# The finishing stage of a graph network: normalisation on ScalarE, wide scaling, earlier weight loads, and moved edge keys

## The chip, the cores and the metric

The kernel runs on one core of a Trainium2 chip. The metric is the device time of one execution in microseconds, as the median of several runs: 5247.54 us for the kernel before, from three runs between 5239.28 and 5250.59 us.

## The reference

A graph of 6250 nodes with 256 features and 100,000 edges sorted by destination goes through two layers. Layer 0 is a graph attention convolution (softmax over the edges of each destination), a linear attention and a mixture of experts. Layer 1, where most of the change lies, is

```python
xn = _layernorm(x, axis=-1)
x = x + _L1_gnn_ref(xn, ...) + _L1_mix_ref(xn[None], ...)[0]
x = x + _L1_ffn_ref(_layernorm(x, axis=-1)[None], ...)[0]

h1 = relu(gcn_conv(embedding, W1, b1, src, dst, n))   # 256 -> 64
h2 = relu(gcn_conv(h1, W2, b2, src, dst, n))          # 64 -> 256
```

A `gcn_conv` multiplies by W, scales a row by `dinv[src] * dinv[dst]` per edge (`dinv` is one over the root of the degree plus one), sums over the edges of each destination, and adds the row's own term and the bias. `_L1_ffn_ref` sends every row to the one expert with the largest gate score, if that expert has a place left (capacity 1.25 times the mean, given out in row order), and scales by the softmax probability.

## The kernel before

The 6250 nodes stand in 49 blocks of 128 rows (`NB`, `P`). The sorted edges are cut in tiles of 128; where a tile covers several blocks, it is repeated once for each, so that every step has one block; there are 832 steps (`NS`), in groups of eight. The stages run one after another, each in a block with a queue of instructions per engine, all engines meeting at its end.

`edge_steps` finds the tile and the block of each step and gathers the source, destination and weight of its edges (`rs`, `rd`, `rw`, each 128 x 896 numbers). VectorE converts the destinations to floats (`fd`), SyncE stores them at L225 as the key rows `key_d`, VectorE subtracts the block's first row (`fl`, L370), and TensorE turns the tables. `project_nodes`, the next stage, begins on VectorE with a wait for nine weight loads, for the stored keys (`m.keyed`) and for three masks of GpSimd (L552 is the last). The keys are read in `score_edges` and compared with their neighbours in `normalise_edges`, where a maximum is taken over each run of edges with equal keys.

`convolve(1)` sums the second graph convolution. GpSimd gathers 782 tiles of source rows, one indirect DMA each (L1886), into a ring; TensorE multiplies them by one-hot matrices that VectorE makes (L2109, L1953), VectorE adds the sums into `m.agg` (L1964), and the mixing network's block work goes between, with one block load per block on SyncE (L1923), after the loads of its weights. VectorE first folds weights (`fold`).

`finish_and_route1` handles the 49 blocks in seven groups of seven (`G`), with these steps, all in program order on each queue:

- VectorE: `scale(k)` multiplies 64 sums by `dinv` into `us` (L2273), five blocks ahead; `finish(k)` takes the relu of the projected block and adds it to the residual rows (L2277); `stats(k)` (L2281); per group `variance`, `choose` for the group before (gate scores to mask, L2316 to L2329), `normalise` (reciprocal L2301, the token's copy L2304, seven normalisations into `disp`, L2308), `place` for the group before (ranks to slots, L2338 to L2361).
- TensorE: `turn(k)` four blocks ahead (L2434), `project(k)` (L2440), then for a block of the group before `turn_normal` (L2447) and one block later `gate` (L2457), and per group the rank and total matmuls of the mask (L2482, L2483).
- ScalarE: copies of turned sums (L2394), of turned normalised rows (L2400) and of the residual rows into `disp` (L2407), per group a square root (L2422) and the exponential of the gate's gaps (L2425). It also issues the loads of the first two experts.
- GpSimd: per group seven indirect DMAs (L2255) that scatter the rows of `disp`, which is double, to the experts' buffer. `disp` is written again when the scatters of the group two before have landed (`sent`).
- SyncE: first four loads (64 x 256 weights `w2` and its bias row, the gate's weights and bias), then the finished rows to the output.

TensorE starts when these four loads have landed. A prologue of four turned blocks and the first group have no gate work; the last turn of the loop (the tail here) has only gate work. I number the seams between groups 0 to 6: at seam g the variance and normalisation are of group g, and choice and placement of group g-1.

## Time and profile before

| | us |
|---|---|
| median of three runs | 5247.54 |
| the runs | 5239.28, 5247.54, 5250.59 |
| profiled execution, its own time | 5253.34 |
| its span in the profile | 5251.4 |
| mean granted TensorE clock, of 1 | 0.736 |
| finishing stage, first instruction to last scatter's issue | 4605 to 4764 |

The profile is of one execution. It gives busy time per engine (PE is TensorE's matmuls, PEld its weight loads, DVE VectorE, ACT ScalarE, POOL GpSimd, SP SyncE; a q behind the name is the queue's own work, such as issuing a DMA), and for each instruction its start, duration, and what ended the idle time before it. An idle time "issue" is one in which the engine waited for nothing that the profile shows. The granted clock is 0.50 when TensorE gets 1.2 GHz and 1.00 at 2.4 GHz.

### The profile page before, as it was taken

The numbers are of one execution on the slowest core, as the hardware profiler recorded it, in microseconds if no ns is written. First come the engines' busy times: TensorE is split into PE (matmuls) and PEld (weight loads), VectorE is DVE, ScalarE is ACT, GpSimd is POOL, SyncE is SP. The second block draws the span as 40 slices with busy tenths as digits, with TensorE's granted clock in tenths as the row PEclk, the third lists the DMA queues.
The fourth block names the chain that finished last, engine by engine and source line by source line (L and its number), as shares of the span: only waits on it lengthen the run. The fifth ranks groups of instructions, "written<-read, shape, count | busy, mean of one in ns | idle before, by whom it ended". The sixth has DMA issues, their size and how long they took to land. (4 is left out here: it accounts for less than half of the span.)

```text
span 5251.4 us, 62217 instructions
## 1 busy us (share of the span) xinstructions
PE 3522.0 (67%) x13908; PEld 2764.9 (53%) x13909; DVE 2526.5 (48%) x5949; ACT 1049.5 (20%) x2215; POOL 3048.2 (58%) x2894
## 2 busy tenths in 40 slices
PE   4866666665399975999655555554555555567998
PEld 3734444433277765888544444443444545455665
DVE  5477777777712553222643444444333333463444
ACT  0122222221199911332100000000000000042111
POOL 1177777777299944222277777776777777722111
PEclk9976677777699987999565666665555555567999
DMA  5398777777588863222511111112111111132221
GB/s 111 115 248 247 241 241 241 241 241 224 158 264 272 272 210 112 70 70 62 166 33 32 33 33 33 33 32 44 33 32 33 33 33 33 30 118 89 73 79 34
DMA packets 437408, 616.97 MB, mean 117 GB/s; under 512 B 104714, under 2 KB 315466, under 8 KB 437003
## 3 DMA queue, kind: packets, MB, share of 16 engines
q1 hardware_dynamic: 306767, 391.02, 23.6%
q0 software_dynamic: 107728, 200.97, 15.6%
q10 hardware_dynamic: 22812, 23.86, 1.7%
q8 instruction: 36, 0.59, 0.0%
q14 instruction: 65, 0.53, 0.0%
HBM read 418.38 MB, written 211.62 MB: 120 GB/s over the span
## 5 line engine op out<-in xcount | busy, mean ns | idle before, releaser
L1886 POOL DMA_INDIRECT big<-t_d,src_tiles x1564 | 1482.6, 948 | 622.9 <-issue 457.3
L2109 PE MATMUL v_bank<-big,v_oh 128*128 x3328 | 685.2, 392 | 914.5 <-POOLq L1882 855.5
L2109 PEld LDWEIGHTS v_bank<-big,v_oh 128*128 128x128 f32 x3328 | 651.8, 300 | 990.9 <-issue 990.8
L704 POOL DMA_INDIRECT big<-xl_d,src_steps x832 | 794.1, 954 | 261.0 <-issue 230.2
L815 PE MATMUL se_z_ps<-big,se_oht 128*128 x1664 | 687.7, 569 | 370.9 <-DVE se_z L744 326.5
L1964 DVE TENSOR_TENSOR big<-big,v_bank 128x64 f32 x1664 | 366.8, 220 | 1138.9 <-PE v_bank L2109 917.5
L815 PEld LDWEIGHTS se_z_ps<-big,se_oht 128*128 128x128 f32 x1664 | 424.2, 276 | 634.1 <-issue 555.2
L1134 POOL TENSOR_TENSOR ae_v<-ae_v,ex 128x2048 f32<-128x2048 f32 x104 | 380.6, 3673 | 109.8 <-DMA ae_v<-xj_d 108.7
L744 DVE TENSOR_TENSOR se_z<-se_z_ps,big 128x528 f32<-128x528 f32 x416 | 291.7, 701 | 279.9 <-DMA big<-xl_d,src_steps 268.7
L1176 PE MATMUL ae_sums<-ae_v,ae_oh 128*128 128x266 f32 x1664 | 396.2, 395 | 25.9 <-ACT ae_oh L1125 17.3
L1176 PEld LDWEIGHTS ae_sums<-ae_v,ae_oh 128*128 128x128 f32 x1664 | 309.1, 191 | 112.9 <-issue 60.7
L2555 POOL DMA_INDIRECT out<-e_y,e_idx x64 | 63.1, 986 | 422.5 <-DVE e_y L2598 407.9
L1631 POOL DMA_INDIRECT y_d<-e_y,e_idx x112 | 117.3, 1047 | 305.8 <-DVE e_y L1620 282.5
L759 DVE TENSOR_REDUCE ex<-se_w 128x512 f32 (+1 forms) x416 | 281.7, 677 | 0.0
L753 DVE SCALAR_TENSOR_TENSOR se_w<-se_z,se_scaled 128x512 f32<-128x512 f32 x416 | 281.2, 676 | 0.1
L784 ACT ACTIVATE se_oht<-se_dlb,se_place 128x1024 f32<-128x1024 bf16 x104 | 119.4, 1148 | 802.8 <-PE se_z_ps L815 695.2
L1122 ACT ACTIVATE ae_oh<-iota,dl_steps 128x128 f32<-128x128 f32 x832 | 254.2, 388 | 40.1 <-PE ae_sums L1176 32.7
L1953 DVE TENSOR_TENSOR v_oh<-v_bank,dl_steps 128x1024 f32<-128x1024 f32 x208 | 253.4, 1219 | 7.9 <-issue 7.8
L2651 PE MATMUL e_bank<-big,e_ht 128*128 128x256 f32 x1024 | 225.3, 381 | 0.7 <-ACT e_ht L2616 0.7
L2640 PE MATMUL e_bank<-e_xt,big 128*128 128x465 f32 (+1 forms) x512 | 215.2, 579 | 1.6 <-DVE e_xt L2574 1.6
L2651 PEld LDWEIGHTS e_bank<-big,e_ht 128*128 128x128 f32 x1024 | 193.2, 190 | 29.6 <-issue 1.6
L2086 ACT ACTIVATE v_ht<-v_bank,c 128x128 f32<-128x128 f32 x98 | 30.7, 364 | 879.7 <-PE v_bank L2140 879.6
(480 smaller groups left out, 4926.0 us busy)
## 6 DMA issues: line engine op xcount, KB each, us to landing
xj_d<-big SPq DMA_DIRECT2D x208, 528.0 KB, 3.3
ae_v<-xj_d SPq DMA_DIRECT2D x208, 528.0 KB
se_dlb<-dlr_d SPq DMA_DIRECT2D x104, 256.0 KB, 5.1
big<-t_d,src_tiles POOLq DMA_INDIRECT x1564
buf_d<-ne_blank SPq DMA_DIRECT2D x4, 4112.0 KB
e_xs<-buf_d SPq DMA_DIRECT2D x56, 258.0 KB, 2.9
big<-xl_d,src_steps POOLq DMA_INDIRECT x832
cp_y<-y_d SPq DMA_DIRECT2D x14, 896.0 KB, 7.3
```

The source lines that it names most:

```text
L704: nc.gpsimd.indirect_dma_start(half_of(u)[:, k, :], None, table, bass.IndirectOffsetOnAxis(ap=m.src[:, t:t + 1], axis=0)).then_inc(landed[ ...
L744: nc.vector.tensor_tensor(z[:, u, k:k + 2, :], z_ps[n % ZB][:, :, 0:LW], xj[:, u, k:k + 2, :], ALU.add).then_inc(s["z_ready"], 1)
L753: nc.vector.scalar_tensor_tensor(w[:, v % 2, :, :], z[:, u, k:k + 2, 0:D], 0.0, wide, ALU.max, ALU.mult).then_inc(s["weighed"], 1)
L759: nc.vector.tensor_reduce(m.ex[:, bass.ds(q * 2 * H, 2 * H)], w[:, v % 2, :, :].rearrange("p k (h c) -> p (k h) c", h=H), AX.X, ALU.add)\
L815: last = nc.tensor.matmul(z_ps[n % ZB][:, i, 0:LW], oht[:, u, k + i, :], of_block(m.xr, blocks[2 * (v % 2) + i]), start=True, stop=True)
L1122: nc.scalar.activation(oh[:, w % 2, k, :], m.iota[:, :], ACT.Abs, bias=m.dl[:, bass.ds(g * GS + k, 1)], scale=-1.0).then_inc(s["oh_apart"], 1)
L1134: nc.gpsimd.tensor_tensor(x, x, exps(g).unsqueeze(3).to_broadcast([P, GS, H, HC]), ALU.mult).then_inc(s["scaled"], 1)
L1176: nc.tensor.matmul(of_block(sums, to[k])[:, 0:AW], oh[:, w % 2, k, :], v[:, w, k, :], start=False, stop=True, skip_group_check=True).then_ ...
L1886: nc.gpsimd.indirect_dma_start(rows[:, t % RING, :], None, table, bass.IndirectOffsetOnAxis(ap=m.srct[:, t:t + 1], axis=0)).then_inc(lande ...
L1964: V.tensor_tensor(of_block(m.agg, blocks[k]), of_block(m.agg, blocks[k]), bank[u][:, k * MH:(k + 1) * MH], ALU.add).then_inc(s["added"], 1)
L2109: last = nc.tensor.matmul(bank[u][:, k * MH:(k + 1) * MH], oh[:, u, k, :], of_block(rows, at[k]), start=True, stop=True)
L2651: last = nc.tensor.matmul(y_ps[(UT * v + t) % 2][:, 0:D], ht[:, f, t * P:(t + 1) * P], w2[:, u, f, :], start=(f == 0), stop=(f == FC - 1))
```

## The change

- In `edge_steps` GpSimd computes, after the local positions `fl` are there, `runs = fd + 8192 * (fl - clamp(fl, 0, 127))` in four operations of 128 x 896, and SyncE stores `runs` as the key rows, behind its other stores. So an edge that isn't in the step's block gets a key of its own. The wait for the stored keys moves from VectorE at the start of `project_nodes` to SyncE at its end.
- The weights `w2`, `wg`, `bg` of the finishing stage live in buffers that `convolve(1)` shares; it clears `w2` on VectorE first and issues the four loads on SyncE ahead of its block loads, and waits for them at its end.
- `scale` takes seven blocks at once (`us` has two groups), before the loop for groups 0 and 1, then after each group's variance for the group after the next.
- `normalise` on VectorE ends with the reciprocal, the token's copy and `shift = -mean * rstd`; ScalarE does the seven normalisations as Identity activations with a bias and a scale per partition, after its exponential. GpSimd waits for them before a group's scatter.

```diff
@@ edge_steps, SyncE
-                sp.wait_ge(floats, 1)
-                sp.dma_start(m.key_d.rearrange("(j p) e -> p j e", p=P), fd[:, :, :]).then_inc(m.keyed, 16)
...
+                sp.wait_ge(told, 4)
+                sp.dma_start(m.key_d.rearrange("(j p) e -> p j e", p=P), runs[:, :, :]).then_inc(m.keyed, 16)
@@ edge_steps, GpSimd
+                pool.wait_ge(floats, 3)
+                nc.gpsimd.tensor_scalar(inside[:, :, :], fl[:, :, :], 0.0, float(P - 1), ALU.max, ALU.min).then_inc(told, 1)
+                pool.wait_ge(told, 1)
+                nc.gpsimd.tensor_tensor(runs[:, :, :], fl[:, :, :], inside[:, :, :], ALU.subtract).then_inc(told, 1)
+                pool.wait_ge(told, 2)
+                nc.gpsimd.tensor_scalar(runs[:, :, :], runs[:, :, :], 8192.0, None, ALU.mult).then_inc(told, 1)
+                pool.wait_ge(told, 3)
+                nc.gpsimd.tensor_tensor(runs[:, :, :], runs[:, :, :], fd[:, :, :], ALU.add).then_inc(told, 1)
@@ project_nodes, SyncE's end and VectorE's start
+                sp.wait_ge(m.keyed, 16)
...
-                dve.wait_ge(m.keyed, 16)
@@ convolve
+                    sp.wait_ge(s["emptied"], 1)
+                    sp.dma_start(m.last_w2[0:MH, :], a["L1_gnn_W2"]).then_inc(s["later"], 16)
+                    sp.dma_start(m.last_w2[MH:MH + 1, :], a["L1_gnn_b2"].rearrange("(a n) -> a n", a=1)).then_inc(s["later"], 16)
+                    sp.dma_start(m.last_wg[:, :, :], a["L1_ffn_gate_w"].rearrange("(c p) n -> p c n", p=P)).then_inc(s["later"], 16)
+                    sp.dma_start(m.last_bg[:, :], a["L1_ffn_gate_b"].partition_broadcast(P)).then_inc(s["later"], 16)
...
+                if which == 1:
+                    sp.wait_ge(s["later"], 64)
...
+                if which == 1:
+                    V.memset(m.last_w2[:, :], 0.0).then_inc(s["emptied"], 1)
@@ finish_and_route1, GpSimd and VectorE
+                    pool.wait_ge(s["xn_ready"], G * (g + 1))
...
+                V.memset(us[:, :, :, MH:P], 0.0).then_inc(s["ones"], 1)
+                dve.wait_ge(s["ones"], 1)
+                V.memset(us[:, :, :, MH], 1.0).then_inc(s["ones"], 1)
+
+                def scale(g):
+                    part = slice(G * g, G * g + G)
+                    if g >= 2:
+                        dve.wait_ge(s["ut_made"], G * (g - 1))
+                    V.tensor_tensor(us[:, g % 2, :, 0:MH], m.agg[:, part, :], m.dinv[:, part].unsqueeze(2).to_broadcast([P, G, MH]),
+                                    ALU.mult).then_inc(s["u_ready"], 1)
...
-                    for i in range(G):
-                        k = G * g + i
-                        V.tensor_scalar(disp[:, g % 2, i, 0:D], rows_of(k), m.mean[:, k:k + 1], m.rstd[:, k:k + 1],
-                                        ALU.subtract, ALU.mult).then_inc(s["xn_ready"], 1)
+                    V.scalar_tensor_tensor(shift[:, part], m.mean[:, part], -1.0, m.rstd[:, part], ALU.mult, ALU.mult).then_inc(s["shifted"], 1)
...
                         variance(g)
+                        if g + 2 < NGR:
+                            scale(g + 2)
                     if g >= 1:
                         choose(g - 1)
@@ finish_and_route1, ScalarE
+                def normal(g):
+                    act.wait_ge(s["shifted"], g + 1)
+                    if g >= 2:
+                        act.wait_ge(sent[g % 2], 16 * G * (g // 2))
+                    for i in range(G):
+                        k = G * g + i
+                        nc.scalar.activation(disp[:, g % 2, i, 0:D], rows_of(k), ACT.Identity, bias=shift[:, k:k + 1],
+                                             scale=m.rstd[:, k:k + 1]).then_inc(s["xn_ready"], 1)
...
                         nc.scalar.activation(gap[:, :, :], gap[:, :, :], ACT.Exp).then_inc(s["exped"], 1)
+                    if g < NGR:
+                        normal(g)
@@ finish_and_route1, TensorE
-                pe.wait_ge(s["weights"], 64)
-                pe.wait_ge(s["ones"], 3)
+                pe.wait_ge(s["ones"], 2)
```

## Rows read from the trace of the kernel before

**Rows 1.** Page, part 5: line, engine, operation, count | busy, mean ns | idle.

```profile
L1886 POOL DMA_INDIRECT big<-t_d,src_tiles x1564 | 1482.6, 948 | 622.9 <-issue 457.3
```

**Rows 2.** Stretches: start:end, length, busy time (count) by engine, clock, DMA, GB/s.

```profile
4605.00:4765.00 160.00, 106.81 (x518) 92.36 (x518) 96.20 (x410) 64.51 (x173) 49.83 (x59) 0.65 0.34 109
...
4724.00:4737.00 13.00, 13.00 (x54) 11.56 (x52) 5.58 (x20) 5.22 (x15) 6.90 (x7) 0.50 0.22 75
```

**Rows 3.** Timeline of VectorE: start, us, operation, idle before and releaser.

```profile
4652.09 0.42 DVE L2277 SCALAR_TENSOR_TENSOR big<-fr_bank,big 128x256 f32<-128x256 f32 x1 [1.65 <-PE fr_bank L2440]
...
4671.00 0.42 DVE L2277 SCALAR_TENSOR_TENSOR big<-fr_bank,big 128x256 f32<-128x256 f32 x1 [0.41 <-PE fr_bank L2440]
```

**Rows 4.** Timeline of all engines where the finishing stage starts.

```profile
4605.06 0.27 DVE L2265 MEMSET fr_us<- 128x256 f32 x1 [1.12 <-PEq L136]
...
4609.84 0.93 PEld L2434 LDWEIGHTS fr_bank<-ident,fr_us 128*128 128x128 f32 x4 [9.64 <-DMA fr_bg<-in_L_ffn_gate_b]
```

**Rows 5.** Timeline of VectorE: a wide scaling; then the first group's blocks.

```profile
3589.67 0.62 DVE L2022 TENSOR_TENSOR big<-big,dinv 128x448 f32<-128x448 f32 x1
...
4616.31 0.23 DVE L2273 TENSOR_SCALAR fr_us<-big,dinv 128x64 f32<-128x64 f32 x1
...
4616.46 0.41 DVE L2277 SCALAR_TENSOR_TENSOR big<-fr_bank,big 128x256 f32<-128x256 f32 x1
```

**Rows 6.** Timeline of all engines between groups 2 and 3.

```profile
4657.18 0.22 DVE L2316 TENSOR_TENSOR fr_score<-fr_bank,fr_bg 128x56 f32<-128x56 f32 x1 [0.47 <-PE fr_bank L2457]
...
4659.04 2.35 DVE L2308 TENSOR_SCALAR fr_disp<-big,mean,rstd 128x256 f32<-128x256 f32 x7
...
4659.61 0.25 ACT L2425 ACTIVATE fr_gap<-fr_gap 128x56 f32<-128x56 f32 x1
...
4661.31 0.20 DVE L2338 COPY fr_tot<-fr_bank 128x56 f32<-128x56 f32 x1
...
4664.18 0.42 DVE L2277 SCALAR_TENSOR_TENSOR big<-fr_bank,big 128x256 f32<-128x256 f32 x1
...
4665.98 0.98 PEld L2457 LDWEIGHTS fr_bank<-fr_wg,fr_xt 128*128 128x128 f32 x4
```

**Rows 7.** Groups of ScalarE's instructions by line and shape.

```profile
L1122 ACT ACTIVATE ae_oh<-iota,dl_steps 128x128 f32<-128x128 f32 x832 | 254.2, 388 | 40.1 <-PE ae_sums L1176 32.7 <-PEq L136 7.4
...
L1651 ACT ACTIVATE e_ht<-e_bank,big 128x256 f32<-128x256 f32 x224 | 94.0, 471 | 115.3 <-PE e_bank L1674 115.3
...
L2400 ACT COPY fr_xt<-fr_bank 128x256 f32<-128x256 f32 x49 | 18.3, 373 | 37.9 <-PE fr_bank L2447 37.9
...
L2425 ACT ACT_TABLE_LOAD x6 | 7.7, 1283 | 0.1
```

**Rows 8.** Timeline of ScalarE: eight activations in a row.

```profile
1429.70 2.44 ACT L1122 ACTIVATE ae_oh<-iota,dl_steps 128x128 f32<-128x128 f32 x8 [7.37 <-PEq L136]
```

**Rows 9.** Timeline of VectorE at the seam after group 3.

```profile
4678.85 0.17 DVE L2304 COPY fr_disp<-fr_token 128x7 f32<-128x7 f32 x1 [2.09 <-DMA buf_d<-fr_disp,slots]
```

**Rows 10.** Timeline of all engines in the tail.

```profile
4739.20 0.25 ACT L2425 ACTIVATE fr_gap<-fr_gap 128x56 f32<-128x56 f32 x1
...
4740.97 0.93 PEld L2457 LDWEIGHTS fr_bank<-fr_wg,fr_xt 128*128 128x128 f32 x4 [0.44 <-ACT fr_xt L2400]
...
4751.68 0.22 DVE L2338 COPY fr_tot<-fr_bank 128x56 f32<-128x56 f32 x1 [1.19 <-PE fr_bank L2483]
```

**Rows 11.** Page, part 5: GpSimd's multiplication of two inputs.

```profile
L1134 POOL TENSOR_TENSOR ae_v<-ae_v,ex 128x2048 f32<-128x2048 f32 x104 | 380.6, 3673 | 109.8 <-DMA ae_v<-xj_d 108.7
```

**Rows 12.** Timeline of VectorE at the end of the edge preparation.

```profile
73.46 1.44 DVE L370 TENSOR_SCALAR big<-big,es_boff 128x128 f32<-128x128 f32 x7
...
82.81 0.23 DVE L563 TENSOR_SCALAR pn_attl<-pn_attm,pn_attc 128x8 f32<-128x8 f32 x1 [1.19 <-POOL pn_attm L552]
```

**Rows 13.** Timeline of all engines at the second convolution's start.

```profile
3612.59 20.94 SPq L1923 DMA_DIRECT2D v_xt<-xnt_d  x2
...
3630.99 2.02 PE L2140 MATMUL v_bank<-v_xt,m 128*128 128x128 f32 x8
```

More of the change, by code:

```diff
@@ L160, in edge_steps @@
         junk = m.ex[:, NT:2 * NT]
+        inside = m.ex[:, 2 * NT:2 * NT + SPAD].rearrange("p (j e) -> p j e", e=P)
+        runs = m.ex[:, 2 * NT + SPAD:2 * NT + 2 * SPAD].rearrange("p (j e) -> p j e", e=P)
         sval = sb("sval", [P, SJ])
@@ L191, in edge_steps @@
         turned, turnedback, chain = m.sem("es_turned"), m.sem("es_turnedback"), m.sem("es_chain")
-        identset = m.sem("es_identset")
+        identset, told = m.sem("es_identset"), m.sem("es_told")
         tilesin, tilesf = m.sem("es_tilesin"), m.sem("es_tilesf")
@@ L1872, in convolve @@
             s.update({n: m.sem("v1_" + n) for n in ("ht_made ht_ready out_made xn_ready xb_ready mixed res_ready "
-                                                    "fold_in chain kvt t_made t_back m2_made folded").split()})
+                                                    "fold_in chain kvt t_made t_back m2_made folded emptied later").split()})
             mixed = s["ht_made"]
@@ L2184, in finish_and_route1 @@
         NGR = NB // G
-        w2, ut, us = sb("w2", [P, D]), sb("ut", [P, 4, P]), sb("us", [P, 4, P])
-        wg, bg = sb("wg", [P, KC, NE]), sb("bg", [P, NE])
+        w2, wg, bg = m.last_w2, m.last_wg, m.last_bg
+        ut, us = sb("ut", [P, 4, P]), sb("us", [P, 2, G, P])
+        shift = sb("shift", [P, NB])
         xt, disp = sb("xt", [P, 4, D]), sb("disp", [P, 2, G, RW])
@@ L2194, in finish_and_route1 @@
         bank = [ctx.enter_context(nc.psum_tensor(f"fr_bank{i}", [P, 512], F32)) for i in range(8)]
-        s = {n: m.sem("fr_" + n) for n in ("weights masks ones u_ready ut_made ut_ready made res_ready stat chain var std xn_ready "
-                                           "xt_made xt_ready g_made g_back l_in exped counted totals t_ready p_ready r_ready slots "
+        s = {n: m.sem("fr_" + n) for n in ("masks ones u_ready ut_made ut_ready made res_ready stat chain var std xn_ready "
+                                           "xt_made xt_ready g_made g_back l_in exped counted totals t_ready p_ready r_ready slots shifted "
                                            "sent0 sent1 experts res_out").split()}
@@ L2214, in _ @@
             def _(sp):
-                sp.wait_ge(s["ones"], 2)
-                sp.dma_start(w2[0:MH, :], a["L1_gnn_W2"]).then_inc(s["weights"], 16)
-                sp.dma_start(w2[MH:MH + 1, :], a["L1_gnn_b2"].rearrange("(a n) -> a n", a=1)).then_inc(s["weights"], 16)
-                sp.dma_start(wg[:, :, :], a["L1_ffn_gate_w"].rearrange("(c p) n -> p c n", p=P)).then_inc(s["weights"], 16)
-                sp.dma_start(bg[:, :], a["L1_ffn_gate_b"].partition_broadcast(P)).then_inc(s["weights"], 16)
                 for g in range(NGR):
@@ L2264, in _ @@
                 V = nc.vector
-                V.memset(us[:, :, MH:P], 0.0).then_inc(s["ones"], 1)
-                V.memset(w2[:, :], 0.0).then_inc(s["ones"], 1)
-                dve.wait_ge(s["ones"], 2)
-                V.memset(us[:, :, MH], 1.0).then_inc(s["ones"], 1)
-                def scale(k):
-                    if k >= 4:
-                        dve.wait_ge(s["ut_made"], k - 3)
-                    V.tensor_scalar(us[:, k % 4, 0:MH], m.agg[:, k, :], m.dinv[:, k:k + 1], None, ALU.mult).then_inc(s["u_ready"], 1)
+                V.memset(us[:, :, :, MH:P], 0.0).then_inc(s["ones"], 1)
[7 more added lines that the diff above has]
+                                    ALU.mult).then_inc(s["u_ready"], 1)
                 def finish(k):
@@ L2361, in place @@
                     V.tensor_copy(disp[:, g % 2, :, RW - 2], m.prob[:, part]).then_inc(s["p_ready"], 1)
-                for k in range(5):
-                    scale(k)
+                scale(0)
+                scale(1)
                 dve.wait_ge(s["masks"], 10)
@@ L2369, in _ @@
                         for k in range(G * g, G * g + G):
-                            if k + 5 < NB:
-                                scale(k + 5)
                             finish(k)
@@ L2430, in turn @@
                 def turn(k):
-                    pe.wait_ge(s["u_ready"], k + 1)
+                    pe.wait_ge(s["u_ready"], k // G + 1)
                     if k >= 2:
                         pe.wait_ge(s["ut_ready"], k - 1)
-                    nc.tensor.matmul(bank[k % 2][:, 0:P], us[:, k % 4, :], m.ident[:, :], start=True, stop=True).then_inc(s["ut_made"], 1)
+                    nc.tensor.matmul(bank[k % 2][:, 0:P], us[:, k // G % 2, k % G, :], m.ident[:, :], start=True, stop=True).then_inc(s["ut_made"], 1)
                 def project(k):
@@ L2733, in build @@
         end_stage(nc, m)
-        for which in range(2):
-            convolve(nc, m, a, which)
+        convolve(nc, m, a, 0)
+        end_stage(nc, m)
+        with ExitStack() as last:
+            m.last_w2 = last.enter_context(nc.sbuf_tensor("last_w2", [P, D], F32))
+            m.last_wg = last.enter_context(nc.sbuf_tensor("last_wg", [P, KC, NE], F32))
+            m.last_bg = last.enter_context(nc.sbuf_tensor("last_bg", [P, NE], F32))
+            convolve(nc, m, a, 1)
             end_stage(nc, m)
-        finish_and_route1(nc, m, a)
+            finish_and_route1(nc, m, a)
         experts1(nc, m, a)
```

## The prediction, made before the change was run

> **What bounds the kernel now.** I read the page first: its costliest groups show the GpSimd queue issuing the second layer's gathers one after another, 1564 of them with an idle time that is nearly all "issue" [rows 1]. The change adds nothing to that queue inside the two convolutions, so about 2,000 us of the kernel can't move. Then I looked for the places the diff touches: the end of the edge preparation (75 to 84 us), the start of the second convolution (from 3602 us) and the finishing stage (4605 to 4765 us). The last is the only one where it matters which engine is late. Its row among the stretches shows no engine full: TensorE 106.8 of 160 us, VectorE 96.2, ScalarE 64.5, at a mean granted clock of 0.65 [rows 2]. So I read it in order of time. Inside a group of seven blocks TensorE is the bound: VectorE waits 1.65 us per block for the projection at the low clock and 0.41 us at the high one [rows 3]; as its own work between is the same, a block costs 1.24 us more at the low clock. Between two groups TensorE starves while VectorE does variance, gate choice, normalisation and slot placement in one line. That seam, which occurs six times with a choice in it, is what the change works on.
>
> **Start of the finishing stage (gain 3.0 us).** TensorE's first matmul starts at 4609.84, released by the last weight load [rows 4]. With the weights loaded a stage earlier it waits for VectorE: one memset of 896 elements a partition, taken in proportion to 0.27 us for 256 [rows 4] as 0.95 us, a memset of ones (about 0.1 with its wait), and the first seven-block scaling, 128x448 with a broadcast second operand, 0.62 us as an operation of that shape and kind took [rows 5]. From 4605.06 that is 4606.7, and some 0.1 us for the release: 3.0 us earlier. If the wide memset costs nothing it is 3.9, so the bounds are 3.0 and 3.9.
>
> **First group (gain 1.0 us).** Here VectorE is the bound at the high clock: the scaling starts 0.15 us before the finishing operation it is queued ahead of, with no idle between [rows 5]. Seven blocks without it save 1.0 us, or nothing if TensorE can't follow at that pace, which no row shows; I take 1.0, since it now waits on VectorE. The grouped scalings (0.62 us each) come back at five seams and are counted there.
>
> **Seams of groups 1 to 5 (gain 7.1 us).** Take the seam at 4657. Before: the gate scores arrive after VectorE idled 0.47 us; then choice, seven normalisations in 2.35 us from 4659.04, placement from 4661.31, the finishing operation of the next block at 4664.18, and TensorE gets to that group's first gate at 4665.98 [rows 6]. After: the seven-block scaling (0.62 us) sits ahead of the choice; 0.47 us of it fills the idle time, so choice and mask end about 0.2 us later. Placement no longer waits for the normalisations but for the rank and total matmuls. On VectorE's queue, in a seam where nothing covers them, mask to placement is 1.2 us [rows 10], so it begins at 4660.3 instead of 4661.31 and saves 1.0; the per-block scaling ahead of the finishing operation saves another 0.16. Gain on VectorE 1.2 us. The new wait on GpSimd, for normalised rows before each group's scatter, is met long before the slots are, and nothing is queued behind it that is needed sooner. ScalarE must keep up: its exponential ends at 4659.86 [rows 6], then come seven Identity activations with two per-partition operands. No row shows one. With one such operand a 256-wide activation took 471 ns, a copy of that size from PSUM without one 373 ns, so each operand costs about 0.10 us and two give 0.57 us [rows 7]. In a row, eight of 388 ns took 2.44 us, so each overlaps the one before by 0.09 [rows 7, 8]: seven take 0.57 + 6 x 0.48 = 3.45 us. Bounds: 2.4 us (as copies of 0.37 with that overlap times seven, rounded up) and 4.0 (no overlap). They end at 4663.3. Behind them on ScalarE are the evacuation of the next sum and of the first turned block, so the gate's operand is ready by 4664.0; TensorE, released by VectorE, gets to that gate 1.2 us earlier than before, at 4664.75. So ScalarE is hidden by 0.7 us, and it decides from 0.1 us more per activation on. This is five seams; but in one, VectorE waits 2.09 us for a scatter of two groups before [rows 9], in another less. Placement starts the scatter that the next seam waits for, so this is a loop of its own, 14.7 us from a placement's end, just ahead of 4664.18 [rows 6], to the landing at 4678.85 [rows 9]. There the whole 2.35 us of normalisation leaves it and a 0.17 us operation comes in: 2.0 us and, for the shorter wait, 1.5. Sum: 3 x 1.2 + 2.0 + 1.5 = 7.1. The same loop caps what quicker groups can give: with the placement itself (2.8 us) and the 0.3 ahead of it a seam can't follow another in less than 17.8 us.
>
> **Seam 0 (loss 0.6 us).** There is no choice and placement in this one, so VectorE has nothing to win that TensorE waits for, and the wide scaling is ahead of the reciprocal. ScalarE's 3.45 us end after the 2.35 us that they replace, and the first gate waits for the copy queued behind them: 0.6 us later.
>
> **Tail (loss 2.4 us).** The last group's turned rows wait for nothing else. Before, exponential at 4739.20, first gate at 4740.97 [rows 10]. After, ScalarE's first copy starts at 4739.45 + 3.45 = 4742.9 and the first gate at 4743.35; from there the same seven gates and five turns are left, so everything to the last scatter is 2.4 us later (1.3 if the seven take 2.4, 3.0 if 4.0).
>
> **Key rows (loss 0.7 us).** GpSimd gets two two-input and two one-input operations of 896 elements after VectorE's subtraction, done at 74.9. Its two-input rate is 3673 ns for 2048 [rows 11]: 1.6 us each. For the one-input ones half of that to all of it. With waits, 75.1 + 5.2 to 6.8, and SyncE's issue of the store (0.4): 80.7 to 82.3, where VectorE's last work of the stage ended at 81.62, 1.19 us ahead of its next [rows 12]; the stage can't be left until the store is issued. So 0 to 0.9, and more if VectorE's operations get in the way; I take 0.7, near the upper end, as the nearest row is the two-input one. VectorE's dropped wait for that store gains nothing: its first instruction of the next stage was released by GpSimd's mask [rows 12]. The store now comes behind the others on SyncE's queue; the same bytes are done by the same time, and the next stage's end waits for it with 100 us to spare. The Trainium skill ("GPSIMD Engine Reference", 4.1 Engine selection) has one-input work at about line rate and recommends VectorE for two-input work, "~2x slower" here; by its line rate the one-input ones would take 0.9 us each and this term would be near 0. No row here shows such an operation unobstructed.
>
> **Moved loads (0).** Four loads, some 1.9 us of SyncE's time, now stand ahead of the first block load of the second convolution, issued at 3612.59; its matmul ran at 3630.99 [rows 13]. Cover 16 us less the landing. The moved memset (0.27 us) hides ahead of VectorE's wait for the fold's inputs, which are issued up to 3612. If that cover were gone it would be 2.2 us once.
>
> **Sum.** -3.0 -1.0 -7.1 +0.6 +2.4 +0.7 = -7.4 us. The profiled execution took 5253.34 (span 5251.4), so 5245.9 for it; it lies 5.8 us above the median of 5247.54, which makes 5240.1. The three runs reach over 11 us, so a measurement can tell about 0.2% (10.5 us) from no change, and the forecast lies inside that.
>
> **Rivals.**
> - *The clock rises sooner.* TensorE's low-clock stretches after each seam lasted between 4 and over 13 us with the same work; one group never left 0.50 [rows 2]. With less idle time at the seams it could rise earlier. Of the 35 blocks in groups 1 to 5 about 18 ran low; if seven more ran high, 7 x 1.24 = 8.7 us: about 5231. The loop of the scatters (17.8 us) bars much more. For it: the seams carry idle TensorE time that shrinks by half. Against it: 1.9 us of it, in the choice, stays. 23%.
> - *ScalarE becomes the bound.* If an activation costs 0.1 to 0.2 us more than estimated, or Identity needs a table load after the exponential (1.28 us as the others [rows 7]), seams give 0.5 less each and tail and seam 0 lose 1.3 more each: 5240 + 5 = 5245. The trace has Identity behind a logarithm's table without a load, and copies behind both tables used here. 12%. The Trainium skill ("ScalarE: Activation LUTs", Rules for kernel authors) says to keep multiply and add on VectorE; by it the move is a loss wherever ScalarE is the last. The trace agrees for seam 0 and the tail, 3.45 against 2.35, and not for the seams between, where VectorE is last.
> - *The clock stays low* (the other side). If no group after the first reached the high clock, the some 17 blocks in groups 1 to 5 that ran high now would cost 1.24 us more each: +21 - 7 = +14, 5254 to 5262. It decides from six blocks on that lose the high clock, where the forecast's gain is gone, and passes +0.2% from fifteen. For it: group 6 [rows 2]. Against: nothing in the change thins TensorE's work. 5%.
> - *The change doesn't do what it says*, the first matmul being held by something else at the start (a mask of GpSimd, the barrier): 3 us less, 5243. 5%.
>
> **How the numbers follow.** Forecast 5240.1, 55%, its own range 5233 to 5247 with the bounds above and the runs' spread. The range of 8 in 10 takes in the early clock and the ScalarE case and some of the noise: 5227 to 5251. Faster by over 0.2% (under 5237): the early clock nearly whole and a fifth of the forecast, 0.33. Slower (over 5258): the low clock, mostly, and noise, 0.05. Within: 0.62.
>
> **What would show it.** First matmul of the stage 1.7 us after VectorE's first memset, not 4.8. Placement 1.2 us after the mask in every seam. Seven activations in 3.4 us behind each exponential, without a table load between. First gate of a group released by VectorE's finishing operation, not by ScalarE; in the tail, by ScalarE, some 3.9 us after the exponential ends. The stage's length without clock luck 152 to 154 us against 160. The key rows done at about 82 us. Wrong would be: a table load, activations over 0.6 us apart, longer waits for scatters than the 2.09 us now, or any change in the pace of the gathers.

## The result and the profile after

| | before | changed |
|---|---|---|
| median of 17 runs each, us | 5247.81 | 5256.61 |
| their range | 5239.28 to 5253.34 | 5245.62 to 5261.39 |
| span of the profiled execution | 5251.4 | 5258.5 |
| its mean granted clock | 0.736 | 0.732 |

The ratio is 1.0015, 95% interval 1.0009 to 1.0022: the change costs 8.8 us (4.7 to 11.5). The forecast was a gain of 7.4 us, and the median lies above the forecast's range.

Stage by stage, from the first instruction of one to that of the next, the two profiles differ at five places:

| stage | before | changed | difference |
|---|---|---|---|
| edge preparation, end of | 81.99 | 86.45 | +4.5 |
| edge scoring | 1066.6 | 1059.2 | -7.4 |
| first convolution | 1016.0 | 1020.2 | +4.2 |
| second convolution | 1004.1 | 1009.6 | +5.5 |
| finishing stage | 161.0 | 161.5 | +0.5 |

**The edge stage** first. This is the timeline of the changed kernel at its end (start, us, operation, idle before):

```profile
75.06 3.64 POOL L268 TENSOR_SCALAR ex<-big 128x896 f32<-128x896 f32 x1 [6.55 <-DVE big L380]
...
78.78 2.08 POOL L270 TENSOR_TENSOR ex<-big,ex 128x896 f32<-128x896 f32 x1
80.65 1.04 DVE L389 CAST src_tiles<-es_bank 128x512 uint32<-128x512 f32 x2 [0.36 <-PE es_bank L408]
80.95 2.47 POOL L272 TENSOR_SCALAR ex<-ex 128x896 f32<-128x896 f32 x1
83.50 2.07 POOL L274 TENSOR_TENSOR ex<-ex,big 128x896 f32<-128x896 f32 x1
85.60 0.36 SPq L235 DMA_DIRECT2D key_d<-ex  x1
...
87.23 0.23 DVE L573 TENSOR_SCALAR pn_attl<-pn_attm,pn_attc 128x8 f32<-128x8 f32 x1 [5.54 <-POOL pn_attm L563]
```

The four operations take 10.5 us from first start to last end; VectorE is through at 81.7 and sits idle for 5.54 us where it did for 1.19 [rows 12]. In the five kernels with these operations (this one and four below) the next stage begins at 86.4 to 88.9 us, on average 6 us later than in the twelve without. About 1.3 us of that comes from ahead of them: in three of the five VectorE's subtraction, which the clamp waits for, ended at 76.4 to 77.4 us instead of about 74.9, because a row gather landed later (VectorE waited 1.52 us for it in one and 2.48 us in another). Whether the key part has a hand in that is open.

**GpSimd's gathers** are the second thing. These are lines of the changed kernel's page (line, engine, operation, count, then busy us, mean ns, idle us); the mean of the first was 948 ns before [rows 1]:

```profile
L1896 POOL DMA_INDIRECT big<-t_d,src_tiles x1564 | 1492.8, 954 | 622.1 <-issue 453.4
...
L714 POOL DMA_INDIRECT big<-xl_d,src_steps x832 | 786.9, 946 | 261.2 <-issue 219.9
```

The 1564 gathers of the convolutions are the same instructions as before, and take 10.2 us more; the 832 of edge scoring (954 ns before) take 7.2 us less.

**The finishing stage** starts as forecast:

```profile
4611.13 0.81 DVE L2281 MEMSET fr_us<- 128x896 f32 x1 [1.11 <-PEq L136]
...
4611.99 0.67 DVE L2289 TENSOR_TENSOR fr_us<-big,dinv 128x448 f32<-128x448 f32 x1
...
4612.77 0.93 PEld L2459 LDWEIGHTS fr_bank<-ident,fr_us 128*128 128x128 f32 x4 [6.50 <-DVE fr_us L2283]
```

The first weight load comes 1.6 us after the memset, where it took 4.8 [rows 4]. And the seam behind group 2 looks as worked out (compare [rows 6]):

```profile
4662.21 0.22 DVE L2343 TENSOR_TENSOR fr_mask<-fr_mask,fr_valid 128x56 f32<-128x56 f32 x1
...
4662.48 0.68 PE L2506 MATMUL fr_bank<-fr_mask,fr_tri 128*128 128x56 f32 x2 [1.81 <-DVE fr_mask L2343]
...
4663.15 0.25 ACT L2448 ACTIVATE fr_gap<-fr_gap 128x56 f32<-128x56 f32 x1
4663.30 2.55 ACT L2422 ACTIVATE fr_disp<-big,fr_shift,rstd 128x256 f32<-128x256 f32 x5
...
4663.63 0.22 DVE L2352 COPY fr_tot<-fr_bank 128x56 f32<-128x56 f32 x1 [0.88 <-PE fr_bank L2507]
...
4665.54 0.33 ACTq L2442 DMA_DIRECT2D big<-in_L_ffn_w  x1
4665.76 1.08 ACT L2422 ACTIVATE fr_disp<-big,fr_shift,rstd 128x256 f32<-128x256 f32 x2
...
4666.36 0.75 DVE L2294 SCALAR_TENSOR_TENSOR big<-fr_bank,big 128x256 f32<-128x256 f32 x2
...
4666.74 0.24 ACT L2408 COPY fr_ut<-fr_bank 128x128 f32<-128x128 f32 x1
...
4666.93 1.19 PE L2465 MATMUL fr_bank<-last_w,fr_ut 128*128 128x256 f32 x2 [1.08 <-DVE big L2294]
```

Placement follows the mask's end by 1.2 us, seven activations take 3.54 us, without a table load. What then took the gain away shows in the stretches (start:end, length, busy time of PE, PEld, DVE, ACT, POOL, clock, DMA share, GB/s). This is the whole stage:

```profile
4611.00:4772.00 161.00, 121.33 (x518) 105.86 (x518) 77.22 (x325) 86.75 (x222) 49.42 (x59) 0.57 0.33 108
```

VectorE is relieved of 19 us [rows 2], but TensorE is busy for 121.3 instead of 106.8 us with the same 518 matmul entries, at a granted clock of 0.57 instead of 0.65. Two stretches further in, from one fall of the clock to the next:

```profile
4661.40:4678.47 17.07, 14.90 (x56) 12.91 (x57) 7.86 (x34) 10.05 (x27) 6.80 (x7) 0.50 0.53 175
4678.47:4681.88 3.41, 2.50 (x20) 2.22 (x18) 3.13 (x15) 2.75 (x6) 0.00 (x0) 1.00 0.60 200
```

From 4640.9 to 4722.8 us this comes four times over, once per group. In the whole stage 24 us ran at 2.4 GHz; before it was 48.

### The profile page after: what moved, and what is told of

The parts are those of the page before. It is cut to its first block and busy times, and to the rows that moved or that the text cites. A ratio compares the mean times of both kernels' runs of the same rounds, so it can differ in the third digit from the quotient of the medians.

```text
span 5258.5 us, 62188 instructions
## 1 busy us (share of the span) xinstructions
PE 3543.5 (67%) x13908; PEld 2789.5 (53%) x13909; DVE 2506.5 (48%) x5865; ACT 1070.9 (20%) x2264; POOL 3057.5 (58%) x2898
```

## The experiments

Two groups of questions: whether the key part and the finishing part add up, and what sets the gathers and the clock. "Stage" is the finishing stage; "at 2.4 GHz" the sum of the stretches with a granted clock of 1.00 in it. The ratios are to the kernel before as it ran beside them, with medians of 5248.3 to 5250.4 (5251.55, a single time, for the last two runs of group 5 and that of group 6).

**1. Without the key part, the key part alone.** The first takes this out of the changed kernel and stores `fd` as before, the second puts it into the kernel before:

```diff
-                nc.gpsimd.tensor_scalar(inside[:, :, :], fl[:, :, :], 0.0, float(P - 1), ALU.max, ALU.min).then_inc(told, 1)
...
-                nc.gpsimd.tensor_tensor(runs[:, :, :], runs[:, :, :], fd[:, :, :], ALU.add).then_inc(told, 1)
```

> The changed kernel without its edge-key part (GpSimd's four operations gone, the key rows stored at the place and in the form of the kernel before). Theory A, the end of the edge stage hangs on GpSimd and nothing behind makes up for it: the next stage begins at 82.0 us instead of 86.45, the median is 4.4 us below the changed kernel's 5256.6, so about 5252 and still 4 us above before (ratio 1.0008); the finishing stage is 161 us long as in the changed kernel. Rival, the edge stage's delay is absorbed by the stages behind it: no difference beyond 1 us between this and the changed kernel.

> The kernel before with only the edge-key part. Theory A: next stage begins at 86.4 us instead of 82.0, median 4.4 us above before (ratio 1.0008), finishing stage unchanged at about 161 us. Rival (absorbed): ratio 1.0000. The two together with the first run tell whether the two parts of the change add up.

Without the key part the median was 5244.79, ratio 0.9992 (0.9983 to 1.0001), 7 us lower than expected. The key part alone gave 5263.66, ratio 1.0026 (1.0015 to 1.0038), that is +13.7 us where 4.4 were expected. Its edge stage ended 5.9 us later than before, less than half of what it costs. Their pages hold the rest:

```profile
L1886 POOL DMA_INDIRECT big<-t_d,src_tiles x1564 | 1479.4, 946 | 623.2 <-issue 462.8
...
L1896 POOL DMA_INDIRECT big<-t_d,src_tiles x1564 | 1493.2, 955 | 624.2 <-issue 461.7
```

The first line is of the kernel without key operations, the second of the one with nothing but them: 14 us in the convolutions' gathers. The finishing stage of the kernel without the part was 153.3 us long, not 161: the 161.5 of the changed kernel didn't repeat here, though the code of that stage is the same. It came back in three later profiles of this form (161.7 to 162.3).

**2. The normalisation back on VectorE.**

```diff
-                    V.scalar_tensor_tensor(shift[:, part], m.mean[:, part], -1.0, m.rstd[:, part], ALU.mult, ALU.mult).then_inc(s["shifted"], 1)
...
+                        V.tensor_scalar(disp[:, g % 2, i, 0:D], rows_of(k), m.mean[:, k:k + 1], m.rstd[:, k:k + 1],
+                                        ALU.subtract, ALU.mult).then_inc(s["xn_ready"], 1)
...
-                        normal(g)
```

> The changed kernel with the seven normalisations of a group back on VectorE (ahead of placement); early weights, wide scalings and key rows stay. Theory B, the changed kernel's finishing stage gains 9 us at the seams and loses 13 us because TensorE stays at the 1.2 GHz level for 12 of each group's blocks' time: here the seams are 1.1 us longer each but high-clock stretches come back (40 us or more of them in the stage instead of 24), stage 152 to 158 us, median 3 to 9 us below the changed kernel. Rival, the low clock of the groups has nothing to do with where the normalisation is: high clock about 24 us again, stage 161 + 5 = 166 us less 2 for the tail, median 3 us above the changed kernel.

Median 5259.36, ratio 1.0017 (1.0008 to 1.0026): not to be told from the changed kernel, where theory B had 3 to 9 us less. In the profile a seam took 9.46 us from the group's last finishing operation to the next group's first, 1.1 us more than with ScalarE (8.25 to 8.44), as expected; 48 us at 2.4 GHz came with it, and the stage was 157.5 us long. Its tail was no shorter (34.2 us from the last finishing operation to the stage's end), because there VectorE waited 3.7 us for a scatter first. A profile of one execution doesn't tell whether the clock came from the edit.

**3. Keeping TensorE busy.** Six matmuls of 256 columns per group, whose sums nobody reads:

```diff
+                def warm(n, at):
+                    for _ in range(n):
+                        nc.tensor.matmul(at, m.ident[:, :], w2[:, :], start=True, stop=True)
...
+                        if 1 <= g < NGR and k == G * g + 1:
+                            warm(3, bank[6][:, 128:384])
...
+                        if g >= 2:
+                            pe.wait_ge(s["slots"], g - 1)
+                        warm(3, bank[7][:, 256:512])
                         pe.wait_ge(s["counted"], g)
```

> The changed kernel with three matmuls of 256 columns, whose results nobody reads, ahead of each group's mask matmuls and three ahead of the second projection of groups 1 to 6, where TensorE sits idle for 1.8 and 1.1 us per seam. Theory B with the idle time at the seams as the reason for the low clock: the clock stays at 2.4 GHz in most of the stage, groups take 8.1 instead of 12.0 us, stage about 140 us, median some 20 us below the changed kernel. Rival, TensorE's clock in this stage doesn't depend on that idle time: groups stay at 12.0 us, six matmuls at 0.86 us each less the 2.9 us of idle time add 2.3 us per seam, stage about 173 us.

Median 5245.08, ratio 0.9990 (0.9981 to 0.9999), 11.5 us below the changed kernel, key operations and all; the stage was 146.7 us long with 89 us at 2.4 GHz, and a block took 1.32 us nearly everywhere. What is missing to the expected 140 us went into a wait for scatters, at three seams and once more in the tail (4.41 us). This is VectorE at the seam behind group 2:

```profile
4657.10 0.19 DVE L2318 RECIPROCAL rstd<-tmp 128x7 f32<-128x7 f32 x1
4662.53 0.17 DVE L2321 COPY fr_disp<-fr_token 128x7 f32<-128x7 f32 x1 [5.24 <-DMA buf_d<-fr_disp,slots]
```

With groups this quick the scatter of two groups before hasn't landed: this is the loop that the prediction had priced.

**4. Three buffers.** `disp` gets a third buffer in the room of the edge scores (`m.ex`), with a semaphore of its own; `sent[g % 2]` becomes `sent[g % 3]`. With filler, without key part:

> The changed kernel without the key part, with the filler matmuls of the run before and with three buffers for the scattered rows instead of two (the third in room that the edge scores had). In the filler run VectorE waited for a scatter at three seams (12.84, 10.85 and 9.72 us from a group's last finishing operation to the next's first, against 7.8 at one that didn't wait); with three buffers it waits nowhere: 5.0 + 3.0 + 1.9 = 10 us shorter at the seams, and the finishing stage 137 us instead of 146.7. Median: 153.3 (the changed kernel's stage without keys) less 137 = 16 us below the run without the key part (5244.8), so 5229, ratio 0.996 to before. Rival, the waits were only the place where the low clock's loss shows up elsewhere: stage 145 or more.

Median 5216.14, ratio 0.9939 (0.9926 to 0.9953), stage 128.5 us, 92 us of it at 2.4 GHz, five seams of 7.8 us and no scatter wait. That is 8.5 us less in the stage and 13 in the median than expected; the high clock now held for 85 us in one piece, where the waits had left pieces of up to 27. And the buffers without the filler:

> The changed kernel without the key part, three buffers for the scattered rows, no filler. If the buffers alone make the gain: the seams that waited for a scatter (10.36 and 8.13 us in the run without the key part) come down to 7.8, stage 150 us, median 3 us below that run's 5244.8. What is missing to 128.5 us is the filler's: 22 us by the 2.4 GHz level. Rival, the buffers are the larger part: stage below 140 us.

Median 5244.12, ratio 0.9985 (0.9976 to 0.9994), not to be told from the run without the key part (5244.79, 0.9992). The two runs of this experiment differ by the filler alone, so with three buffers the filler is worth 0.9939 against 0.9985, some 24 us. What the filler would do to the kernel before was not tried. The profile without it had the low clock of the changed kernel's again:

```profile
4605.20:4767.00 161.80, 121.84 (x518) 106.31 (x518) 77.42 (x325) 86.65 (x222) 50.16 (x59) 0.57 0.33 108
```

**5. What slows the gathers.** Three edits. The kernel before gets four memsets of one element, or one more semaphore, used by nobody; in the changed kernel the keys are computed by VectorE between its evacuations (`scalar_tensor_tensor` for the last two operations).

> The kernel before with four memsets of one element per partition on GpSimd where the changed kernel has its four key operations, with the same waits and the same semaphore; the key rows are stored as before. The earlier runs showed a gather of the convolutions at 952 ns (median) in each kernel with GpSimd's key operations and at 945 without, and one of the edge scoring at 946 with and 954 without. Theory C, what the queue holds ahead (four more instructions and a semaphore) sets it: 952 and 946 here too, convolutions some 11 us longer in sum and edge scoring 7 shorter than before. Rival, the work itself (two big inputs, 128x896) does it: 945 and 954 as before. The edge stage still ends at 82 us by both.

> The kernel before with one more semaphore allocated in the edge stage, which nobody uses, so that later ones get other numbers. If semaphore numbers set a gather's duration: 952 ns in the convolutions, 946 in edge scoring. If it is the instructions on GpSimd's queue: 945 and 954 as before.

> The changed kernel with the key rows computed on VectorE in three operations (clamp, difference, multiply and add in one), placed between its evacuations, where it waits 0.36 to 0.55 us for TensorE each time; nothing of it on GpSimd. At 0.6 + 1.0 + 1.0 us against 1.6 us of waits the stage ends at 83 to 84.5 us instead of 86.4 to 88.9. By theory C or its rival gathers go back to 945 ns (convolutions) and 954 (edge scoring), since GpSimd's queue is as before. Median: 3 us less for the edge stage and 4 for the gathers in sum: 7 us below the changed kernel, about 5250. If the semaphore did it, 952 and 946 stay and it is 5253.

All three had gathers as the kernel before: 947, 947 and 946 ns in the mean of the convolutions. So it is neither the number of instructions nor the semaphores, but goes with GpSimd's tensor operations. With the keys on VectorE the next stage began at 82.4 us and the median was 5242.15, ratio 0.9994 (0.9985 to 1.0004), 14 us below the changed kernel, where 7 were expected; the finishing stage was 150.1 us. The finishing stage of the memset and semaphore kernels, in the form before, was 164.0 and 164.8 us (single times 5248.28 and 5249.66). Then the size, with operations of one element per partition in the kernel without the key part:

```diff
+                nc.gpsimd.memset(spare, 0.0).then_inc(told, 1)
+                pool.wait_ge(told, 1)
+                nc.gpsimd.tensor_tensor(spare[:, 2:3], spare[:, 1:2], spare[:, 0:1], ALU.subtract).then_inc(told, 1)
```

> The changed kernel without its key part, but with a memset and two operations of the kind tensor-with-scalars (clamp, multiply) of one element per partition on GpSimd at that place. Four memsets left a gather at 945 ns in the convolutions and 954 in edge scoring, the four key operations made it 952 and 946. Theory D, having run operations of this kind is enough: 952 and 946 here, the two convolutions 6.0 and 6.5 us longer than in kernels without (1015.1 and 1003.5), edge scoring 5.7 us shorter. Rival, the size of the operations (128x896) or the two-input kind is what counts: 945 and 954, the stages 1015, 1003.5 and 1064 us. The finishing stage has the changed form: about 155 us, the mean of its three profiles so far (161.5, 153.3, 150.1) against 163.7 for the form before (161.0, 164.9, 164.0, 164.8).

> The same with two operations of the kind tensor-with-tensor instead of the two with scalars. By theory D's other half: 952 and 946 if this kind does it. Against it: the kernel before runs 104 of them in the edge aggregation, ahead of both convolutions, and still has 945 there; then 945 and 954. Finishing stage about 155 us again.

```profile
L1893 POOL DMA_INDIRECT big<-t_d,src_tiles x1564 | 1498.9, 958 | 622.8 <-issue 456.7
...
L1893 POOL DMA_INDIRECT big<-t_d,src_tiles x1564 | 1492.7, 954 | 622.3 <-issue 455.1
```

The first line is of the run with scalar operands, the second of the two-input one: either kind is enough, and with 0.7 us of work on one element the convolutions take over 10 us longer. The convolutions lasted 1025.0 and 1011.4 us, and 1020.3 and 1009.8 (single times 5257.36 and 5246.06). The two-input kind does it although 104 such operations run ahead of the convolutions anyway. That left the place of the first use:

> The changed kernel without its key part, with a memset and two tensor-with-tensor operations of one element per partition on GpSimd at the start of the first convolution. The same three in the edge stage made a gather 952 ns (convolutions) and 946 (edge scoring); GpSimd's own 104 operations of this kind in the edge aggregation leave it at 945. Theory E, what counts is that the kind is used for the first time ahead of edge scoring's and the convolutions' gathers, in the edge stage: here the first use is the aggregation's as in the kernel before, so 945 and 954. Rival, more instructions of this kind anywhere ahead of a convolution slow it: 952 in the convolutions and 954 in edge scoring. Finishing stage about 155 us.

> The same three small operations as the very first on GpSimd's queue in the edge stage, ahead of its first mask, iota and gather. Theory E: as where they stood behind the edge gathers, 952 and 946, if only the stage of first use counts; another pair of values if the order against the first gather counts. Rival (their place right ahead of the stage's end matters): 945 and 954.

```profile
L1891 POOL DMA_INDIRECT big<-t_d,src_tiles x1564 | 1479.2, 946 | 524.9 <-issue 457.0
...
L1892 POOL DMA_INDIRECT big<-t_d,src_tiles x1564 | 1492.0, 954 | 622.7 <-issue 456.6
```

First line: at the start of the convolution, behind the aggregation, no effect. Second: as the first of the edge stage, the full one (single times 5240.92 and 5247.19). For the convolutions both came out as theory E has it, each in one run. For edge scoring theory E fell. The first line here is of the kernel with the operations at the convolution, the second of the same kernel without them:

```profile
L704 POOL DMA_INDIRECT big<-xl_d,src_steps x832 | 786.6, 945 | 259.1 <-issue 220.8
...
L704 POOL DMA_INDIRECT big<-xl_d,src_steps x832 | 792.6, 953 | 259.0 <-issue 221.7
```

Edge scoring was over at 1294 us, and the three operations came at 2572 us: they can't have shortened those gathers by having run. The 21 gathers of the edge stage itself say the same, 944 ns in the median against 952 in the kernel without. So at least part of what sets a gather's duration is fixed in the program as built, before anything runs, and then the place of an edit in time says little. The chip doesn't explain the edge stage's 944: the changed kernel, run again on that chip (6.), had 952 there. Other stages point the same way: in the kernels with the full key operations the last stage's scatters take 969 to 972 ns in the mean and in all others 984 to 986, those with the one-element operations among them. So "first use" names the pattern in the convolutions and not its cause.

**6. The changed kernel once more.**

> The changed kernel once more, for a second profile of the same program. If the length of the finishing stage goes with the 2.4 GHz time that the execution happens to get: between 150 and 162 us with 51 to 24 us at 2.4 GHz, longer by about 0.35 us for each us less (from the eight unfilled profiles of the changed form or the one before). If 24 us is what this program always gets: 161.5 again. Gathers 952 and 946 ns again, edge stage left at 86.4 to 88.9 us.

```profile
4603.10:4752.00 148.90, 105.19 (x518) 91.27 (x518) 77.14 (x325) 86.74 (x222) 49.49 (x59) 0.66 0.36 117
```

The same program took 149.3 us for this stage instead of 161.5, with 48 us at 2.4 GHz instead of 24: 0.51 us for each us less where 0.35 had been expected. (Gathers 955 ns in the mean, edge stage left at 86.4 as before.) The execution took 5239.74, 20.5 us less than the first; 12.2 of them lie in the finishing stage and 8.4 in the stages between edge scoring and the convolutions, where the cause is open.

**7. All parts together.** Keys on VectorE, weights early, wide scaling, ScalarE's normalisation, filler and three buffers:

> All parts of the changed kernel, key rows computed on VectorE, and the filler matmuls and three buffers in the finishing stage. The run without the key part had 5216.1; the keys on VectorE ended the edge stage at 82.4 where kernels without them have 81.2 to 82.0, so 0.7 us more: 5217, ratio 0.994 to before, finishing stage 128.5 us. Rival, the long stretch at 2.4 GHz was luck of one execution: stage 128 to 150 us and a median of 5225 or more.

```profile
4600.30:4728.00 127.70, 98.80 (x596) 83.87 (x596) 77.14 (x325) 86.13 (x222) 50.49 (x59) 0.87 0.42 136
...
4610.00:4700.00 90.00, 79.44 (x512) 66.24 (x510) 65.48 (x280) 76.28 (x193) 34.75 (x35) 1.00 0.56 183
```

5216.11 us, ratio 0.9935 (0.9922 to 0.9949). This version beats both kernels, by 34 us the one before; it holds 1.00 from end to end of the groups, with TensorE busy for 79 of 90 us.

## Why the prediction was wrong

**The key rows, forecast +0.7, are the step that failed, twice.** The first failure is the price of an operation. I took 1.6 us for two inputs and 0.8 to 1.6 for one, in proportion to 3673 ns for 2048 elements [rows 11]. They took 2.08 and 2.07, and 3.64 (clamp, two scalars) and 2.47 (one scalar). The one-input kind is the slower one here; I had put it between half and all of the two-input one. VectorE did the clamp in 0.62 us and the difference in 1.08. The Trainium skill ("GPSIMD Engine Reference", 4.1 Engine selection) has one-input work at about line rate; the runs show four to six times the 0.62 us of VectorE's clamp, and the measurement decides. For two inputs its "~2x slower" agrees (2.08 against 1.08). Interference by VectorE was not it: of the two operations of two inputs the first ran beside VectorE's evacuations and the second after them, at the same price. The upper bound of 0.9 was thus far too low: it was +4.5 in the first pair of profiles and +6 on average.

The second is "the change adds nothing to that queue inside the two convolutions, so about 2,000 us of the kernel can't move." The instructions didn't change, their duration did. With tensor operations on GpSimd in the edge stage (eight profiles) a gather of the convolutions has 952 to 955 ns in the median, without (nine profiles) 944 to 947; the means of the stages, without the run with the small scalar operations, are 1020.9 and 1015.2 us (first convolution), 1009.8 and 1003.8 (second): 12 us. Edge scoring gave back about 6 of them (1058.4 against 1064.7 us; 1056.5 to 1060.3 against 1060.5 to 1070.5). The second mean leaves out the kernel with its operations at the convolution, which had the short gathers here and took 1057.0 us. So the cost is shown as one of having these operations in the program; how it comes about is open. The prediction did list "any change in the pace of the gathers" as a sign of being wrong. No row of the kernel before shows this, and none could; what I could have said is that a step of 1 per cent in a gather is 15 us here and that I had no ground for zero.

**The finishing stage, forecast -8.1, held in its form; one pair of profiles hid it.** The form before had 161.0, 164.9, 164.0 and 164.8 us, mean 163.7. The changed form (two buffers, no filler, ScalarE normalising) had 161.5, 149.3, 153.3, 150.1, 158.0, 154.9, 162.3 and 161.7, mean 156.4: 7.3 less. By the scatter of these single profiles I estimate that difference as good to 4 or 5 us. The time at 2.4 GHz was about the same in the mean, 41 us before and 38 after. Term by term, on profiles of equal clock where it matters:

- Start: -3.0 (first finishing operation 5.23 us after the stage's first instruction instead of 8.23). Forecast 3.0.
- First group: a block took 0.66 us instead of 0.82 at the high clock, six intervals 4.51 instead of 4.93 in the two first profiles, as the clock rose during the group: -0.4 against -1.0. Over all profiles of either form it was 4.93 to 5.60 before and 4.34 to 5.47 after.
- Seams 1 to 5: 9.62 us before; 8.25 to 8.44 with the low clock, 7.8 with the high one: 1.2 to 1.8 each against 1.2. The two scatter waits of before (11.75, 10.22) were absent in the changed kernel's first profile, where the groups were slow; at the high clock they came back (9.92 in the second). Forecast -7.1, measured -9.0 in the first pair of profiles and -7.2 over the four and eight (the five seams 49.5 against 42.3). The parts were not as worked out, so the close sum is partly luck: 3.5 of the 7.1 were for shorter scatter waits, and such waits stood in two profiles of four before and in five of eight after; the rest is a seam gain that grows from 1.2 to 1.8 with the clock.
- Seam 0: from the last finishing operation to the fourth block of the next group 9.42 us before, 9.55 after: +0.1 against +0.6.
- Tail: 31.8 us before, 33.9 after: +2.1 against +2.4. The Trainium skill ("ScalarE: Activation LUTs", Rules for kernel authors) would keep this on VectorE; the trace agrees for the tail, where seven activations of 3.5 us stand ahead of the first copy, and not for the seams between.
- ScalarE hidden by 0.7 us: it isn't. Its copy of the turned sum, behind the activations, ends at 4666.98 and VectorE's finishing operation at about 4666.8; TensorE's projection, which needs both, starts between. The size was right: seven activations took 3.54 us against 3.45. (Its lower bound of 2.4 was misworked; copies of 0.37 with that overlap come to 2.1.)

**The clock** was a rival ("the clock stays low", 5%) that decided what the two profiles seemed to say. In the first profile four groups that had had the high clock early before (1, 3, 4, 5) were 13 us longer in sum, and that hid the whole gain. (Of the 13, 2.2 only make up for seam 0, where the next group's first finishing operation came 2.88 us after the last one instead of 5.07.) But it isn't a property of the change alone: the same program had both 24 and 48 us at 2.4 GHz. The pattern with 17.1 us low and 3.4 high in each group appeared in four of nine profiles of the changed form (three buffers counted), in none of four of the form before; a group then lasts 20.4 us each time. Less idle time alone did not bring the high clock, as the rival "the clock rises sooner" had it: at the seam behind group 2 TensorE sat idle for 1.80 and 2.45 us before and for 1.81 and 1.08 after, in the profile with the lower clock. Whether the changed form falls into the pattern more often is open. The Trainium skill ("TensorE: Matmul & The Clock Gate", Part 1) says of a kernel's start that the same kernel gets its clock after different numbers of matmuls from run to run; the repeated program shows such a difference in the middle of a kernel.

**The sum** by the means over the profiles: +6 edge stage, +12 convolutions, -6 edge scoring, -7.3 finishing stage: +5, where the runs have +8.8 (4.7 to 11.5). For the key part alone +12 against 13.7; for the change without it -7.3 against -4.2 (-8.9 to +0.5). The moved loads cost nothing that shows: the second convolution has the same length with and without them where the gathers are equal (1002.5 to 1005.8 of the six changed forms, 1003.7 to 1004.1 of the three of before).

## What to carry to other kernels

An engine that issues a thousand small operations is sensitive to a per cent in each; an edit elsewhere on the same engine isn't free just because it adds nothing there, and the mean of these operations belongs among the first things compared. Where TensorE's clock moves within a stage, one profile of each kernel compares two draws, so count the time at either level before reading a gain or a loss. And where TensorE starves at seams, a few matmuls for nothing can be worth more than shortening the seam: the stage took 128 us instead of 149 to 162, once the buffers let the groups follow each other.

## What was not expected of the hardware

- GpSimd, 128x896 in 32 bits: clamp with two scalars 3.64 us, multiplication with one 2.47, two inputs 2.07. One element behind the edge gathers: 0.47 to 0.50 us for the first of a kind, 0.19 to 0.23 for the second; but 0.19 for both where they were first in the queue, and 0.19 and 1.62 at the start of the convolution, so no fixed price can be named.
- Two one-element tensor operations on GpSimd in the edge stage make each of 1564 later indirect gathers 7 to 10 ns longer; memsets don't, nor do the same operations at the start of the first convolution. Placed there, they go with gathers 8 ns shorter in two stages that were over before they ran. How they act was not found. That it is the place of code in the program would fit, but it is only argued.
- TensorE at 1.2 GHz for 17 of every 20.5 us although idle for only 1.8 and 1.1 us per group; six more matmuls a group, put in these gaps, held it at 2.4 GHz for 96 us.
